# An unread 192-column full-precision product after each TensorE step ahead of the first exponential

## What is computed

```python
scores = jnp.einsum('bqhd,bkhd->bhqk', q, k) * attn_scale[0]
scores = jnp.where(mask[None, None], -jnp.inf, scores)
attn = jax.nn.softmax(scores, axis=-1)
out = jnp.einsum('bhqk,bkhd->bqhd', attn, v)
```

## Time and profile before

| What | Value |
|---|---|
| Device time, median of 3 runs | 457.44 us (456.29 to 462.58) |
| Device time of the profiled execution | 459.99 us |
| Span of the profiled execution, first to last instruction | 458.0 us |
| Busy: PE / DVE / ACT / POOL | 424.8 / 345.8 / 224.2 / 144.6 us |
| Mean granted TensorE clock | 0.936 of full speed |

### The profile page before, as it was taken

How to read it: one execution, slowest core, us unless ns; L and a number is a source line. 1 busy time by engine, 2 the same in 40 slices (tenths; PEclk the granted TensorE clock), 3 DMA queues, 4 the chain that set the end, 5 groups by cost and what they waited for, 6 DMA issues and landing times.

```text
span 458.0 us, 7639 instructions
## 1 busy us (share of the span) xinstructions
PE 424.8 (93%) x2430; PEld 198.3 (43%) x2430; DVE 345.8 (76%) x977; ACT 224.2 (49%) x301; POOL 144.6 (32%) x251
## 2 busy tenths in 40 slices
PE   5979999999999999999999998999999999999992
PEld 2622222223223232322235434676776666666660
DVE  2849789778897989799975573867598689856864
ACT  3530056446676868677776886232532342323220
POOL 5065235724837654443644433000000000000000
PEclk9985569559999999999999999999999999999998
DMA  4554205520210202000000004333233324433330
GB/s 126 167 209 131 69 4 155 165 83 14 59 36 13 72 3 64 10 2 1 4 2 3 3 2 96 101 108 104 70 99 111 105 71 133 144 122 94 115 97 23
DMA packets 27383, 34.21 MB, mean 75 GB/s; under 512 B 6096, under 2 KB 16464, under 8 KB 27344
## 3 DMA queue, kind: packets, MB, share of 16 engines
q1 hardware_dynamic: 26240, 33.01, 24.1%
q10 hardware_dynamic: 1104, 0.73, 0.6%
HBM read 29.07 MB, written 4.46 MB: 73 GB/s over the span
## 4 chain that ended last, share of the span: by engine, by line
PE 71%; DVE 16%; issue 6%; DMA 3%; ACT 2%; ACTq 1%; POOL 1%; DVEq 0%; POOLq 0%
PE ps L1393 14%; PE ps L1439 12%; PE ps L1309 12%; DVE comb_rows L1033 7%; PE ps L1408 7%; PE ps L1410 7%; PE ps L1409 7%; PE ps L1376 5%; DVE mx L1036 3%; PE ps L1312 2%; PE ps L1323 2%; DMA bk<-in_bk 1%; ACT probs L927 1%; DVE x L1101 1%; DVE mx L1033 1%
## 5 line engine op out<-in xcount | busy, mean ns | idle before, releaser
L927 ACT ACTIVATE probs<-ps 128x1024 f32<-128x1024 f32 (+2 forms) x160 | 144.9, 940 | 65.1 <-PE ps L1376 63.9
L1033 DVE CUSTOM_DVE_ANT_0 comb_rows<-ps,score_mask 128x512 f32<-128x512 f32 (+1 forms) x192 | 117.5, 664 | 20.8 <-PE ps L1309 19.8
L1309 PE MATMUL ps<-rows_k,rows_q 48*128 48x512 bf16 (+3 forms) x384 | 114.0, 372 | 13.5 <-DVE mx L1033 7.7
L966 ACT ACTIVATE rows_q<-ps 128x512 f32<-128x512 f32 x68 | 40.6, 598 | 97.4 <-PE ps L1410 94.8
L1393 PE MATMUL ps<-probs,Vg 128*32 128x512 f32 (+3 forms) x768 | 85.8, 521 | 1.6 <-ACT probs L927 1.1
L1036 DVE TENSOR_REDUCE mx<-ps 128x2 f32<-128x512 f32 (+3 forms) x128 | 70.2, 586 | 13.4 <-PE ps L1312 9.4
L1309 PEld LDWEIGHTS ps<-rows_k,rows_q 48*128 48x128 bf16 x384 | 30.9, 96 | 112.0 <-DVE mx L1033 68.8
L1376 PE MATMUL ps<-rows_q,rows_k 51*128 51x512 bf16 (+3 forms) x384 | 74.6, 345 | 2.0 <-ACT probs L927 1.9
L1408 PE MATMUL ps<-x1hi,w_hi 128*128 128x512 f32 x136 | 74.0, 544 | 0.0
L1247 DVE TENSOR_TENSOR rows_q<-ps,rows_q 128x512 f32<-128x512 f32 x64 | 44.1, 689 | 36.2 <-PE ps L1439 34.9
L1439 PE MATMUL ps<-rows_k,w_down 128*128 128x512 f32 x136 | 69.5, 593 | 0.7 <-DVE rows_k L1252 0.7
(11 more groups left out here) (117 smaller groups left out, 352.4 us busy)
## 6 DMA issues: line engine op xcount, KB each, us to landing
comb_rows<-weights SPq DMA_DIRECT2D x128, 128.0 KB, 2.9
scratch<-oT SPq DMA_DIRECT2D x8, 384.0 KB, 2.7
w_raw<-in_unitT SPq DMA_DIRECT2D x17, 128.0 KB, 2.7
rows_q<-scratch SPq DMA_DIRECT2D x16, 96.0 KB
rows_k<-scratch SPq DMA_DIRECT2D x14, 96.0 KB
w_down<-in_unitT SPq DMA_DIRECT2D x1, 1088.0 KB, 6.9
xT<-in_xT SPq DMA_DIRECT2D x4, 256.0 KB, 6.0
rows_q<-scratch SPq DMA_DIRECT2D x16, 64.0 KB
```

What stands on the lines that cost most here:

```text
L927: act.activation(dst, src, ACT.Exp).then_inc(exps_ready, 1)
L1033: dve.tensor_tensor_reduce(masked_scores[k % 4][:, 0:m], src[:, 0, :], score_mask[:, 0:m], 1.0, LAST, ALU.add, ALU.max, to).then_inc(max_r ...
L1309: mm = pe.matmul(dst[:, at * m:(at + 1) * m], rows_q[f:f + ROWS, s, p + qt * P:p + (qt + 1) * P], rows_k[f:f + ROWS, s, p + k0:p + k0 + m] ...
```

## The change

The first 52 entries of `pe_order` are taken out of the common loop and run in a loop of their own. In it every maximum step, the two tops too, is followed by one float32 product of `wq` (128 x 128) with the first 192 columns of `xT`, into bank 4. Nothing reads it; the first value block starts bank 4 afresh. It carries no wait and signals nothing. `used`, which says which half of the array comes first in an exponential unit, starts at 1 in both versions at the first "e". Everything after the first exponential is issued as before.

```diff
-HOLD = 10
+HOLD, BESIDE = 10, 192
...
+            first_exps = next(k for k, step in enumerate(pe_order) if step[0] == "e")
+            for kind, _, n in pe_order[:first_exps]:
+                max_step(*MSEQ[n])
+                pe.matmul(bank(VALUES, BESIDE), wq[:, :], xT[:, 0:BESIDE], start=True, stop=True)
             used = 1
-            for kind, g, n in pe_order:
+            for kind, g, n in pe_order[first_exps:]:
```

## The result

The changed kernel takes 472.56 us at the median of five executions (469.60 to 507.03). Two of the five, at 502.60 and 507.03 us, lost the clock: the one at 507.03 was profiled and ran nearly the whole stage ahead of the first exponential at 1.2 GHz, and the one at 502.60 has a mean clock as low (0.904 and 0.892; the other three have 0.974 to 0.981). Of these three (469.60, 470.97, 472.56) the ratio to the kernel before (by now five executions, 456.29 to 471.21 us) is 1.0249, 95% interval 1.0173 to 1.0324.

What follows compares the result with a forecast made beforehand. DVE paces the stage before the first exponential; added products make it PE-bound. Stage +15.0, less 0.6 head start and 1.0 clock, gives +13.4, or +9.9 if the second low stretch goes: 470.8 or 467.3, taken as 470 us, range 456 to 479.

Steps and rivals of the forecast that it cites:

- The price of an added product: Behind each of 52 maximum steps on PE: 0.32 us columns, 0.11 load, 0.10 way back, together 0.53 us.
- the way back: On PE, returning from the added product's shape to the unit's: 0.10 us more, ahead of the unit's own load.
- The stage: First rows landed to first exponential: 45.3 us at 2.4 GHz instead of 30.3, 15.0 more; first exponential near 73 us.
- the masked pairs and the tops: Steps using all rows, in the stage at 2.4 GHz: masked pairs of 128 2.6 us, of 256 3.0, two tops 0.5.
- The bound: In the stage the wait goes from PE's loads to DVE; DVE's busy share falls from 0.9 to about 0.6.
- the head start: DVE's up to two reductions in hand at the first exponential, none with slower PE: 0 to 1.2 us back, 0.6 taken.
- the rival at 453 to 457 us: Added products' and units' loads hidden, 512-column step 0.53 us on PE, DVE keeps 0.61, stage near 30 us; chance 10%.
- The fallen clock: Rival: clock falls near 31 us, steps run at 1.2 GHz, stage 72.4 us, about 499 us in all; chance 12%.
- The clock's worth behind the stage: Low-clock stretches 58.3 to 65.2 and 82.3 to 102.8 us, priced by DVE's busy share: 1.0 and 3.5 us back.

Runs made afterwards that it cites:

- the second product: Changed kernel with 12 HOLD products and two added products of 192 columns behind each of the 52 steps: 490.77 us, single execution.
- bfloat16 variant: Changed kernel with 12 HOLD products, each added product one bfloat16 product of 128 rows and 448 columns instead of float32: 459.62 us, ratio to before 1.0002.
- HOLD = 12: Changed kernel with 12 HOLD products instead of 10 ahead of the first maximum unit: 478.60 us median of four, ratio to before 1.0376.
- last experiment paragraph: No new run: existing profiles compared from first exponential product to last exponential; ten profiles on one line give 0.3 us per us at half speed.
- HOLD = 10: The changed kernel unaltered: 472.56 us median of the first five executions; run once more, 503.49 and 510.48 us.
- half-array variant: Changed kernel, HOLD 12: 64-row, 256-column products in the unused array half behind 42 units, 128-row bfloat16 ones behind masked pairs and tops: 460.03 us, ratio 0.9988.
- bare steps behind 12 HOLD products: Kernel before with 12 HOLD products instead of 10 and no added products: 464.20 us median, ratio 1.0048.

## Why the prediction was right, and where it was off

**The price of an added product** was right: 0.53 us predicted from rows of other shapes, 0.53 measured (28.47 to 29.00), and a step of 0.84 against 0.85. Its parts stood up separately: the second product adds only its columns, 0.33; behind units the half-array product runs beside its neighbour and has no price; the bfloat16 variant lacks the 0.10 of the way back that the earlier trace rows showed for float32 records.

**The stage** was 45.3 us predicted, 44.0 measured where the clock held (28.1 to 72.1), the first exponential at 72.1 against "near 73", both with HOLD = 12. That is +13.7 for the stage instead of +15.0. Most of the missing 1.3 us lies in the masked pairs and the tops: from their start to their added product they take 0.55, 0.65 and 0.11 us, where 0.64, 0.74 and 0.27 had been counted.

**The bound moved as said**: DVE went from busy 0.9 of the stage to 0.72 (31.75 of 44.00), more than the 0.6 named. I counted about 26 us of DVE work; with a slower PE the reductions stand apart instead of overlapping, and two more of 512 columns (22 against 20) fall inside the stage, which is the head start that the prediction priced at 0 to 1.2 us.

**The time**: 470 predicted; the three executions in which the clock held took 469.6 to 472.6. That it came so close is partly luck, for with the same stage at full clock HOLD = 12 took 473.75 to 479.28 us. By their mean clocks (0.974 to 0.981) the three spent about 18 to 25 us at half speed in all, the profiled execution with HOLD = 12 about 45 (0.953 of 477.2 us); at 0.3 us each (last experiment paragraph) that is most of the difference. The prediction had left most of this term at before's level.

**The rule of the Trainium skill that spoke against it** (page "TensorE: Matmul & The Clock Gate", "Part 2: What happens when you issue a matmul": loads are pulled ahead where row groups do not conflict or the load goes to a background buffer) gave the rival at 453 to 457 us. For 128-row products between 48-row units the trace says no: 0.11 us is lost on the way in, in both types. The Trainium skill's own condition on row groups, in the same place, fits where it is met: with the added product in the other half of the array both products and their loads start at 36.38 us and the unit's pace stays at 0.61.

**The fallen clock was given 12%, and that was the step that failed.** Its mechanism and nearly its size were right (about 499 us predicted, stage 72.4; measured 502.6 to 510.5, stage 74.2; an added product took 0.94 us, not 0.85), but it came in four of seven executions. I had read the standstill ahead of the first unit from one profile of before, 27.3 to 28.0 us, and weighed it against stretches at full clock that had none. In the two profiles of the changed kernel with HOLD = 10 the standstill was 1.34 and 1.37 us, mainly because HOLD began at 18.07 and 18.03 us instead of 18.58; the first unit, released by the landing of its rows, started at 28.16 against 28.04. So the length of the wait was never a constant of the kernel, and a bound from its spread belonged into the chance. Whether the executions that kept the clock had a shorter standstill is not shown, since none of them was profiled.

**The clock's worth behind the stage was too small.** I priced 27 us at half speed at 1.0 + 3.5 us, 0.17 us each, by DVE's busy share; the profiles show about 0.3. Nor did the part behind the first exponential get shorter as the sum had it: in the profile with HOLD = 12 it takes 405.2 us against 399.7 before, with a clock of 0.91 against 0.94 in the stretches above. DVE's density at full clock was the wrong yardstick: in the four rows above DVE's busy time is the same (178.35 to 179.53 us) while PE's goes from 197.87 at 0.99 to 211.94 at 0.91, which suggests that the pace there is PE's as well as DVE's. That PE's growth is what sets the time is argued, not shown. Whether the added products make later falls more or less likely is open: behind the stage the changed kernel had 0.92 and 0.95 in its two profiles, with HOLD = 12 0.91, the bfloat16 variant 0.99, before 0.94, and each is one execution.

**What remains of the idea.** Holding the clock in this stage, all through (bfloat16 variant) or nearly so (half-array variant), can be had for nothing (1.0002 and 0.9988, intervals across 1), but by these ratios it buys nothing either: the stage took 32.6 and 29.0 us against 30.3, for DVE's work is still to be done at either clock.

## What to carry to other kernels

An idle TensorE is not free room: on this kernel an extra product cost its columns, plus a load wherever its rows clashed with those of its neighbours, plus 0.10 us behind float32 records; that was 0.53 us for 0.32 us of columns in a gap of 0.29. Put filler in the half of the array that the neighbour leaves alone, or keep its whole price within the gap, as the bfloat16 product nearly did with 0.30, and ask first whether the engine to be sped up sets the pace at all. When a filler's use depends on a clock that must already be high when it begins, look at the spread of the wait ahead of it, not at one trace.

## What the runs showed of the hardware that was not expected

PE busy 71.90 of 71.90 us, with a 128-row float32 product in every step, did not bring the clock back from 0.50; steps of the same instructions begun at 1.00 held it for 44 us. So for the same work both levels lasted, 1.47 and 0.84 us a step. What differed ahead of it in the profiles was 1.3 us of standstill, or 2.5 us, against none; that this alone decides is not shown. Nor is a standstill needed for a fall: the bare steps behind 12 HOLD products lost the clock without one.
